# Clipping the second context attention's exponentials in two steps, on GpSimd and VectorE, with the floor's part added on TensorE

## What is computed

```python
B, Nq, Cq, H, Nkv = 4, 256, 128, 16, 1601      # D = Cq // H = 8, CLAMP = 10000.0
q = (query @ Wq + bq).reshape(B, Nq, H, D).transpose(0, 2, 1, 3)
k = (key_value @ Wk + bk).reshape(B, Nkv, H, D).transpose(0, 2, 1, 3)
v = (key_value @ Wv + bv).reshape(B, Nkv, H, D).transpose(0, 2, 1, 3)
attn = jnp.einsum('bhqd,bhkd->bhqk', q, k) * scale
attn = jnp.clip(attn, -CLAMP, CLAMP)
attn = jax.nn.softmax(attn, axis=-1)
attn = jnp.where(jnp.any(jnp.isnan(attn)), 1.0 / Nkv, attn)
x = jnp.einsum('bhqk,bhkd->bqhd', attn, v).reshape(B, Nq, Cq)
```

## Time and profile before

| | us |
|---|---|
| median of three runs | 4215.71 |
| profiled execution, its own time | 4216.03 |
| its span in the trace | 4213.9 |
| first clip of the stage starts | 1776.4 |
| last clip starts | 2267.9 |
| one clip (L1853) | 1.216 |
| one maxima reduction (L1830) | 1.411 |

### The profile page before, as it was taken

The page is one execution under the profiler, slowest core; times in us unless marked ns, Lnnn a source line. Parts: engine busy times, 40 slices in busy tenths (PEclk is TensorE's granted clock), DMA queues, the critical chain, the costliest instruction groups (busy, mean ns, idle before and its releaser), DMA issues. The chain is left out here.

```text
span 4213.9 us, 58452 instructions
## 1 busy us (share of the span) xinstructions
PE 3324.0 (79%) x23817; PEld 1729.3 (41%) x23826; DVE 2949.0 (70%) x3979; ACT 1853.5 (44%) x2093; POOL 430.3 (10%) x255
## 2 busy tenths in 40 slices
PE   6799999999999975777775886666654669378579
PEld 3433333333333333444443654322322347254357
DVE  4477777777777767699996565599997444546642
ACT  2365565556556543244443143344442236145233
POOL 0000000000000000100000124144441000000000
PEclk9899999999999987799998898656666889599789
DMA  2000000000000000100000201000000110000010
GB/s 84 10 16 8 8 11 13 8 8 13 11 8 8 8 7 7 26 15 9 9 1 16 109 2 35 15 0 0 0 0 0 42 41 1 19 31 1 1 41 6
DMA packets 21597, 68.42 MB, mean 16 GB/s; under 512 B 5201, under 2 KB 5713, under 8 KB 20434
## 3 DMA queue, kind: packets, MB, share of 16 engines
q1 hardware_dynamic: 21330, 64.69, 5.2%
HBM read 49.07 MB, written 0.52 MB: 12 GB/s over the span
## 5 line engine op out<-in xcount | busy, mean ns | idle before, releaser
L1220 PE MATMUL banks<-L0x_ring,L0x_context_rows 128*101 128x512 f32 x1600 | 734.7, 602 | 4.0 <-ACT L0x_ring L1268 4.0
L1279 ACT COPY L0x_ring<-banks 128x1024 f32<-128x1024 f32 (+1 forms) x416 | 387.1, 982 | 536.4 <-PE banks L1208 536.4
L1208 PE MATMUL banks<-L0x_q_thirds,L0x_context_thirds 32*128 32x512 f32 x4800 | 596.2, 608 | 10.3 <-DVE L0x_q_thirds L1385 5.3
L1310 DVE TENSOR_TENSOR L0x_ring<-L0x_ring,L0x_greatest 128x2048 f32<-128x2048 f32 (+1 forms) x208 | 469.9, 2268 | 10.8 <-ACT L0x_ring L1279 9.4
L1326 DVE TENSOR_TENSOR L0x_maxima<-L0x_maxima,L0x_ring 128x1024 f32<-128x1024 f32 (+1 forms) x288 | 322.8, 1162 | 202.8 <-ACT L0x_ring L1279 202.7
L1220 PEld LDWEIGHTS banks<-L0x_ring,L0x_context_rows 128*101 128x101 f32 x1600 | 253.9, 167 | 456.0 <-issue 448.9
L1268 ACT ACTIVATE L0x_ring<-L0x_ring 128x2048 f32<-128x2048 f32 (+1 forms) x208 | 386.4, 1858 | 16.6 <-DVE L0x_ring L1310 16.2
L1208 PEld LDWEIGHTS banks<-L0x_q_thirds,L0x_context_thirds 32*128 32x128 f32 x4800 | 238.1, 186 | 348.4 <-issue 308.1
L1771 ACT ACTIVATE L1x_probs<-banks 128x2048 f32<-128x2048 f32 (+1 forms) x112 | 196.5, 1755 | 252.0 <-PE banks L1705 210.2
L1830 DVE TENSOR_REDUCE L1x_maxima<-banks 128x3 f32<-128x1203 f32 (+1 forms) x176 | 241.4, 1372 | 31.1 <-PE banks L1663 31.1
L1853 DVE SCALAR_TENSOR_TENSOR L1x_probs<-L1x_probs,L1x_floor 128x1024 f32<-128x1024 f32 (+1 forms) x208 | 252.1, 1215 | 11.4 <-ACT L1x_probs L1771 11.1
(11 more groups left out here) (954 smaller groups left out, 5269.8 us busy)
## 6 DMA issues: line engine op xcount, KB each, us to landing
L0x_q_thirds<-L0x_q_context SPq DMA_DIRECT2D x180, 64.0 KB, 2.0
L1f_expert_weights<-in_L1f_experts SPq DMA_DIRECT2D x16, 512.0 KB, 9.5
L2f_expert_weights<-in_L2f_experts SPq DMA_DIRECT2D x8, 512.0 KB, 5.7
L3a_expert_weights<-in_L3a_experts SPq DMA_DIRECT2D x8, 512.0 KB, 6.0
L3f_expert_weights<-in_L3f_experts SPq DMA_DIRECT2D x8, 512.0 KB, 6.2
L1x_k<-L1x_k_rows SPq DMA_DIRECT2D x64, 50.0 KB
L0x_context_thirds<-in_context_thirds SPq DMA_DIRECT2D x1, 2496.0 KB, 14.3
L1x_context<-in_context SPq DMA_DIRECT2D x4, 600.4 KB, 4.6
```

What stands on the lines that cost most here:

```text
L1208: mm = pe.matmul(k.ps[:, score_bank(s) + i, :], thirds[group_rows(i), slot, t, :], q_thirds[group_rows(i), u // 2 % 2, t, :], start=t == 0 ...
L1220: mm = pe.matmul(k.ps[0:CW, bank, :], rows1[0:height(j), j, :], ring[0:height(j), s % RING, i, :], start=s == FIRST[u] and i == 0, stop=s ...
L1279: act.copy(ring[0:r, s % RING, 2 * p:2 * p + len(pair), :], k.ps[0:r, bank:bank + len(pair), :]).then_inc(copied, 1)
L1310: dve.tensor_tensor(o, o, greatest[:, u % 2, None, :].broadcast_to([P, len(js), 512]), ALU.subtract).then_inc(shifted, 1)
```

## The change

The clip is split. GpSimd subtracts the floor from the exponentials in place, one instruction for each tile (208 in all, 128x1024, two inputs in SBUF). VectorE then clips the difference to 0 and 1 with a tensor_scalar in place, which has one tensor input. What the subtraction took away is given back on TensorE: at each unit's last tile four more matmuls multiply the floor by the sum of the values of all tiles. That sum (`v_sums`) is made on VectorE by `add_tiles`, once for each batch, by a reduction of 12 tiles and one addition for the thirteenth. `L1x_probs` gets a third place for a pair. VectorE's clip comes one tick later in its order, `values` one pair later in TensorE's, the copy of a unit's sums two ticks later in ScalarE's.

```diff
+THREE = 3
+COPY_AT = 2
+ADD_TILES_AT = 10
...
+                    if j == JT - 1:
+                        pe.wait_ge(all_tiles, b + 1)
+                        for h in range(4):
+                            pe.matmul(k.ps[32 * h:32 * h + VW, 7, 0:S], v_sums[:, b % 2, 4 * g + h, :],
+                                      floor[:, u % 2, h * S:(h + 1) * S], start=False, stop=False)
...
-                if n == PAIRS[PAIR[n]][-1]:
-                    values(PAIR[n])
+                if n == PAIRS[PAIR[n]][-1] and PAIR[n]:
+                    values(PAIR[n] - 1)
+            values(len(PAIRS) - 1)
...
-                    if at >= 2:
-                        act.wait_ge(summed, at - 1)
+                    if at >= THREE:
+                        act.wait_ge(summed, at - THREE + 1)
...
+            for n in range(TICKS):
+                u, j = divmod(n, JT)
+                p = PAIR[n]
+                o = probs[0:height(j), p % THREE, n - PAIRS[p][0], :]
+                pool.wait_ge(taken, SLOT[("pair", p)] + 1)
+                pool.tensor_tensor(o, o, floor[0:height(j), u % 2, :], ALU.subtract).then_inc(lowered, 1)
...
-                dve.wait_ge(taken, SLOT[("pair", p)] + 1)
-                o = probs[0:height(j), p % 2, n - PAIRS[p][0], :]
-                dve.scalar_tensor_tensor(out=o, in0=o, scalar=1.0, in1=floor[0:height(j), u % 2, :], op0=ALU.min, op1=ALU.max).then_inc(clipped, 1)
+                dve.wait_ge(lowered, n + 1)
+                o = probs[0:height(j), p % THREE, n - PAIRS[p][0], :]
+                dve.tensor_scalar(o, o, 0.0, 1.0, ALU.max, ALU.min).then_inc(clipped, 1)
+
+            def add_tiles(b):
...
+                dve.tensor_reduce(v_sums[:, b % 2].rearrange("p h e -> p (h e)"), v[:, b % 2, 0:full].rearrange("p j h e -> p (h e) j"),
+                                  X, ALU.add).then_inc(full_tiles, 1)
+                dve.wait_ge(full_tiles, b + 1)
+                dve.tensor_tensor(v_sums[0:JLAST, b % 2], v_sums[0:JLAST, b % 2], v[0:JLAST, b % 2, full], ALU.add).then_inc(all_tiles, 1)
...
-                clip(n)
+                if n:
+                    clip(n - 1)
```

More of the change, by code:

```diff
@@ L1602, in attend_clipped @@
     d, H, G = 8, 16, 4
-    k_rows, kT, v, probs, floor, mx, nm, low, qs, yT, rden = bufs
+    k_rows, kT, v, v_sums, probs, floor, mx, nm, low, qs, yT, rden = bufs
     U = len(X_UNITS)
@@ L1720, in values @@
                             pe.wait_ge(copied, u)
+                    if j == JT - 1:
[3 more added lines that the diff above has]
+                                      floor[:, u % 2, h * S:(h + 1) * S], start=False, stop=False)
                     for h in range(4):
                         mm = pe.matmul(k.ps[32 * h:32 * h + VW, 7, 0:S], v[0:height(j), b % 2, j, 4 * g + h, :],
-                                       probs[0:height(j), p % 2, i, h * S:(h + 1) * S], start=j == 0, stop=j == JT - 1)
+                                       probs[0:height(j), p % THREE, i, h * S:(h + 1) * S], start=j == 0, stop=j == JT - 1)
                 mm.then_inc(summed, 1)
@@ L1807, in _ @@
                 u, i = divmod(n, JT)
-                if i == 0 and u:
+                if i == COPY_AT and u:
                     copy(u - 1)
@@ L1850, in clip @@
                 p = PAIR[n]
-                dve.wait_ge(taken, SLOT[("pair", p)] + 1)
-                o = probs[0:height(j), p % 2, n - PAIRS[p][0], :]
-                dve.scalar_tensor_tensor(out=o, in0=o, scalar=1.0, in1=floor[0:height(j), u % 2, :], op0=ALU.min, op1=ALU.max).then_inc(clipped, 1)
+                dve.wait_ge(lowered, n + 1)
+                o = probs[0:height(j), p % THREE, n - PAIRS[p][0], :]
+                dve.tensor_scalar(o, o, 0.0, 1.0, ALU.max, ALU.min).then_inc(clipped, 1)
+            def add_tiles(b):
+                if b:
+                    dve.wait_ge(part_taken, 4 * b)
+                else:
+                    dve.wait_ge(taken, SLOT[("values", 0)] + 1)
+                if b >= 2:
+                    dve.wait_ge(summed, PAIR[JT * G * (b - 1) - 1] + 1)
+                full = JT - 1
+                dve.tensor_reduce(v_sums[:, b % 2].rearrange("p h e -> p (h e)"), v[:, b % 2, 0:full].rearrange("p j h e -> p (h e) j"),
+                                  X, ALU.add).then_inc(full_tiles, 1)
+                dve.wait_ge(full_tiles, b + 1)
+                dve.tensor_tensor(v_sums[0:JLAST, b % 2], v_sums[0:JLAST, b % 2], v[0:JLAST, b % 2, full], ALU.add).then_inc(all_tiles, 1)
             def context_sum(b):
@@ L1870, in _ @@
                     add(u + 1)
-                clip(n)
+                if n:
+                    clip(n - 1)
                 for m in bursts_in(n):
                     reduce_(m)
+                if i == ADD_TILES_AT and u % 4 == 3 and u // 4 + 1 < B:
+                    add_tiles(u // 4 + 1)
+                if n == ADD_TILES_AT:
+                    add_tiles(0)
                 if i == GATHER_AT and u + 1 < U:
@@ L1877, in _ @@
                     context_sum(u // 4 + 1)
+            clip(TICKS - 1)
             for t in range(TILES):
@@ L1907, in layer1_context @@
         low = k.sb("L1x_minus_max", [P, 2, TPB, P], ctx=ctx)
-        probs = k.sb("L1x_probs", [P, 2, 2, 4 * S], ctx=ctx)
+        probs = k.sb("L1x_probs", [P, THREE, 2, 4 * S], ctx=ctx)
+        v_sums = k.sb("L1x_value_sums", [P, 2, H, VW], ctx=ctx)
         mask = probs[:, 0, 0, :].bitcast(I32).rearrange("p (t n) -> p t n", t=TILES)
-        bufs = (k.sb("L1x_k_rows", [P, CTX], ctx=ctx), kT, v, probs,
+        bufs = (k.sb("L1x_k_rows", [P, CTX], ctx=ctx), kT, v, v_sums, probs,
                 k.sb("L1x_floor", [P, 2, 4 * S], ctx=ctx), k.sb("L1x_maxima", [P, 2, len(ITEMS)], ctx=ctx),
```

5 lines of the change are left out of this document (3 added, 2 removed).

## The result

The changed kernel takes 4374.59 us, the median of four runs (4368.98 to 4377.82), against 4215.91 for the kernel before in the same session: a ratio of 1.0374, with a 95% interval of 1.0356 to 1.0392. It is slower, as forecast, and inside the range of 4250 to 4385; but it rose by 158.7 us where 104.9 were forecast. A third of the loss was not foreseen. The profiled execution took 4373.50 us, its span 4371.8.

The account below looks back on a forecast made before the run. GpSimd was taken as the changed loop's bound: 206 tiles x 2.89 us and the ends make 601.6 us against 492.7, +108.9, less 4 for the code load; 4216.0 + 104.9 gives 4321 us, range 4250 to 4385.

Parts of the forecast that it names:

- the exclusion: Attention stage: GpSimd's subtraction and VectorE's clip wait for each other, adding 0.55 us to a 2.34 us tile.
- the moved code load: Expert layer: GpSimd's code load moves to the attention stage's start, giving back 4 us, bounds 0 and 6.2.
- the forecast's own bound: Upper bound: 3.11 us a tile (2.34 + 0.08 + 0.69) and no code-load gain, 4370 us.
- The prediction's other reckoning: Attention stage, by the port rule's letter: a tile costs 2.34 + 0.69 = 3.03 us, some 4350 us in all.
- What is late next: Attention loop: VectorE's 2.10 us and TensorE's 1.84 fit in the 2.89 us tick; GpSimd is the bound throughout.
- the rival without exclusion: Subtraction and clip overlap freely; GpSimd alone sets the pace at 2.34 us a tile, 4208 us; chance 0.12.
- at best 384 us: Attention stage with only VectorE's clip shortened: TensorE is next, so 492.7 us falls to at best 384.
- The clock: Rival: TensorE's clock falls as its busy share drops; at half the clock throughout, 4393 us; chance 0.07.
- Lost turns: Rival: GpSimd always goes first and VectorE clips only when pairs run out, +390 us, 4604 us; chance 0.05.
- What the prediction said would show it: Profile signs: GpSimd nearly always busy, subtractions 2.9 us apart, clips over 0.69 us, reductions at 1.41, TensorE at full clock.

Follow-up runs that it names:

- e3: The changed kernel with a clip that also writes an accumulator, 1.21 us in place of 0.68: 4267.43 us, ratio 1.0115.
- e4: The kernel before with 208 added GpSimd subtractions on tiles of their own that nobody waits for: 4417.03 us, ratio 1.0472.
- e8: The kernel before with one added 16-column GpSimd subtraction at the start of the attention stage, for the code load: 4210.73 us, ratio 0.9985.
- e1: The changed kernel without VectorE's clip, `values` waiting for GpSimd's subtraction: 4257.99 us, ratio 1.0095.
- e10: The changed kernel without GpSimd's subtraction and with the sums of the values replaced by one copy of 256 columns: 4213.25 us, ratio 0.9994.
- e9: The kernel before with only the clip changed, to a tensor_scalar with 0 and 1 that reads no floor: 4209.36 us, ratio 0.9984.
- e2: The changed kernel without GpSimd's subtraction, the short clip kept: 4244.39 us, ratio 1.0061.
- e11: The changed kernel with the sums of the values replaced by one copy of 256 columns: 4357.95 us, ratio 1.0339.
- e5: The changed kernel with each subtraction cut into two instructions of 512 columns: 4376.28 us, ratio 1.0378.
- e6: The changed kernel without VectorE's 128x8 tensor_scalar that clamps the maxima at the turn to the next unit: 4379.29 us, ratio 1.0381.
- e12: The changed kernel with one clip of 2048 columns for each pair of tiles, 112 in place of 208: 4383.97 us, ratio 1.0395.

## Why the prediction was right, and where it fell short

**Right.** The sign, the exclusion and the range. The two engines take turns (e3, e4); GpSimd is busy for 551.9 of its 654.8 us; an undisturbed subtraction takes 2.34 us (2.33 to 2.35 measured); the reductions stay at 1.41; the moved code load gives 4 us (3.9 in the traces of the changed kernel and of e8), the rest lost as forecast to VectorE's instructions, which now end the stage: L2376 took 2.07 us beside GpSimd, and 0.29 before.

```profile
2467.65 2.12 POOL L2848 TENSOR_TENSOR L1f_rows_rest<-z_rows,L1f_rows_in_parts 128x1024 f32<-128x1024 f32 x1 [41.50 <-ACT L1f_rows_in_parts L2841]
2467.84 2.07 DVE L2376 TENSOR_TENSOR L1f_onehot<-L1f_onehot,L1f_key 128x128 f32<-128x128 f32 x1
```

That the time lies in the range is partly luck. It is 10 us below the upper end, 4385, and above the 4370 that the forecast's own bound gives; the range was widened for a clock that falls now and then, and the 3.13 us a tile that nearly equal the bound's 3.11 are made of other things than the bound's whole clip on GpSimd.

**The size of the exclusion** was right as a sum and wrong in its make-up. The forecast was 206 x 0.55 = 113 us, and e3 gives 109. But GpSimd was held up by only 551.9 - 484.5 = 67 us (0.32 a tile). The other 39 are waits of GpSimd for exponentials (103.2 us against 88.8 - 24.6 = 64.2 in e3), which fits a wait that travels from VectorE's queue over the scan, the fill and ScalarE back to GpSimd. The prediction's other reckoning, 2.34 + 0.69 a tile with 4350 us, charged the whole clip to GpSimd. The measured time is 25 us above even that, and since e3 has the exclusion at 109 / 206 = 0.53 us a tile, a little under the 0.55 of the forecast, what is missing is not exclusion.

**What failed is the step "What is late next".** It said that all else fits into VectorE's and TensorE's slack and that GpSimd never waits, so the kernel without exclusion was put at 4208 us. e1 shows 4258 and e3 4267. The forecast's error of 53 us is made up, by the ratios, of 40.0 + 8.4 = 48 us (e1 against the -8.4 of the rival without exclusion), 8.5 (e3 against e1: a clip in company) and -4 (the exclusion). Two terms in it are known:

- *The ring.* VectorE's busy share of 30.11 in 31.0 us was read as the bound, with TensorE's 24.13 next and "at best 384 us". The clip and the reduction did fill the tick, but the ring of reduction and scan has the same 2.47 us. So GpSimd's 2.34 us a tile could not become the pace: e10, which has neither the subtraction nor the sums, lies at -3 us, 6 above the -8.4. e9 measured the relief at 7 us instead of up to 109. What was needed stood in the code: the scans have one set of banks. The trace hid it, since the earlier trace rows has only 31.1 us of idle time before the reductions: the clip covered the rest.
- *`add_tiles`.* Forecast as 3.4 us, hidden; it takes 5.54 us (5.50 in e2, without GpSimd), and 2.15 more for an addition that takes 0.42 in e2 and waits for GpSimd here. Its reads lie far apart, which is the likely reason for the higher price; no run has the same reduction without the stride. It stands between a reduction and the next, on the ring: 28 us in e10 and 15 in e11.

These are 28 + 6 of the 48 us, if the sums cost in e1 what they cost in e2. The remaining 14 us are the distance of e1 (+40) from e2 (+26), and they stay open: e1 has 35 waits of GpSimd in the loop, and no run took them apart. TensorE's clock is a candidate that no run excludes: it is 0.96 in e1 and in e2, and 0.99 in e10. Nor is it shown which of the changed kernel's waits could be removed; e5, e6 and e12 each took one kind away, and none gained.

**The rivals.** Without exclusion: the condition was created in e3, and it lies at +48 us, not at -8. So the change would have lost even on engines that don't disturb each other. The clock: it did fall to 0.86, where the prediction gave this 0.07 and its forecast the full clock, and the rival's 4393 us are not far off. But e3 shows that its fall in the stage comes with the exclusion, and its own share of the loss is not shown. Lost turns: e5's two clips of over 10 us show that they happen there; in the changed kernel the longest clip took 2.84 us and the median 1.51.

**What the prediction said would show it.** Subtractions and clips over their own lengths, reductions at 1.41 and the first GpSimd instruction of the expert layer right behind the cast: all so. GpSimd busy nearly all the time: 333.75 of 400 us, so no; and TensorE at the full clock: no.

## What to carry to other kernels

A busy share near 100% does not make an engine the only bound: before its work is moved away, follow the loop's other dependences (a single buffer between two engines makes a ring) and see how long they take without it. A VectorE tensor_scalar or an instruction with two inputs in SBUF did not run beside GpSimd's subtraction here: 0.53 us of a 0.68 us clip was lost for each tile, since what stands behind the clip in VectorE's queue waits too. A slower form of the instruction can be the faster one in company: the clip of 1.21 us made the kernel 107 us faster than that of 0.68. Work done "once a batch" is not free where it stands between two links of the ring: four sums cost 28 us.
